# A projection stage with products on zeros before its first chunk, one weight taken in quarters, and the next chunk's transposes one tile later

## The reference

```python
xn = _layernorm(x, axis=-1)                                  # x: (2, 2048, 512), float32
q, k, v = (proj(Wq, bq), proj(Wk, bk), proj(Wv, bv))         # x @ W + bias, 16 heads of 32
scores = jnp.einsum('bhqd,bhkd->bhqk', q, k) / jnp.sqrt(jnp.float32(HD))
scores = jnp.where(causal, scores + bias, jnp.finfo(scores.dtype).min)
ctx = jnp.einsum('bhqk,bhkd->bhqd', softmax(scores), v)
attention = ctx.reshape(b, s, d) @ Wo + bo
logits = (norm_w * (xf * jax.lax.rsqrt(var + EPS))) @ router_w.T      # eight experts, the top two
a = jax.nn.silu(jnp.einsum('td,edf->tef', flat, gate_w)) * jnp.einsum('td,edf->tef', flat, up_w)
y = jnp.einsum('ted,te->td', jnp.einsum('tef,efd->ted', a, down_w), cw) * SCALE
return x + attention + y
```

## Time and profile before

| | |
|---|---|
| median of 3 runs | 1926.42 us (1925.46 to 1926.46) |
| profiled execution | 1924.57 us, of which 1922.8 us are its span from first to last instruction |
| PE busy | 1870.5 us (97%) |
| DVE, ACT, POOL busy | 1506.5 (78%), 1415.9 (74%), 1406.0 us (73%) |
| mean granted PE clock | 0.99 |

### The profile page before, as it was taken

How to read it: one execution, slowest core, us unless ns; L and a number is a source line. 1 busy time by engine, 2 the same in 40 slices (tenths; PEclk the granted TensorE clock), 3 DMA queues, 4 the chain that set the end, 5 groups by cost and what they waited for, 6 DMA issues and landing times. The chain is left out here.

```text
span 1922.8 us, 39426 instructions
## 1 busy us (share of the span) xinstructions
PE 1870.5 (97%) x8656; PEld 1441.3 (75%) x8657; DVE 1506.5 (78%) x3497; ACT 1415.9 (74%) x2790; POOL 1406.0 (73%) x1214
## 2 busy tenths in 40 slices
PE   6999999999999999999999999999998989999997
PEld 5788777777777777777777777777756767888875
DVE  6454466898999989999999998999957956666664
ACT  4333322999999999999999999999972235555554
POOL 5111113899999999999999999999948846666665
PEclk9999999999999999999999999999999999999998
DMA  8577767542423424234242342423217756556553
GB/s 274 199 245 257 270 221 235 143 106 63 107 74 77 106 63 110 71 78 104 63 111 70 79 103 63 119 63 83 77 41 230 251 178 122 103 104 108 104 98 65
DMA packets 119242, 242.14 MB, mean 126 GB/s; under 512 B 17632, under 2 KB 54368, under 8 KB 112896
## 3 DMA queue, kind: packets, MB, share of 16 engines
q1 hardware_dynamic: 101120, 205.84, 36.7%
q0 software_dynamic: 18080, 35.81, 10.2%
HBM read 139.28 MB, written 104.21 MB: 127 GB/s over the span
## 5 line engine op out<-in xcount | busy, mean ns | idle before, releaser
L1175 POOL TENSOR_TENSOR probs_lo<-probs,probs_hi 128x512 fp32r<-128x512 f32 x812 | 1020.2, 1300 | 79.4 <-ACT probs L1210 76.4
L1209 ACT ACTIVATE probs_hi<-s_ps 128x512 fp32r<-128x512 f32 x967 | 680.9, 704 | 26.1 <-DVE s_ps L1282 22.2
L1210 ACT ACTIVATE probs<-s_ps 128x512 f32<-128x512 f32 x933 | 637.5, 702 | 10.2 <-DVE s_ps L1282 6.6
L1261 DVE TENSOR_REDUCE m_part<-m_ps 128x1 f32<-128x512 f32 x744 | 477.8, 682 | 3.0
L1518 PE MATMUL s_ps<-q_st,k_st 100*128 100x512 f32 (+3 forms) x880 | 310.5, 385 | 1.1 <-DMA q_st<-m_rows 0.8
L1502 PE MATMUL m_ps<-k_st,q_st 98*128 98x512 f32 (+2 forms) x840 | 291.1, 382 | 1.3 <-DVE v_raw L776 0.8
L1537 PE MATMUL o_ps<-probs_hi,v_split 128*96 128x512 f32 (+3 forms) x741 | 272.4, 375 | 1.7 <-POOL probs_lo L1175 1.7
L1538 PE MATMUL o_ps<-probs_lo,v_split 128*96 128x512 f32 (+3 forms) x741 | 273.8, 371 | 0.0
L1258 DVE CUSTOM_DVE_ANT_0 m_ps<-m_ps,mask_row 128x128 f32<-128x128 f32 x496 | 244.4, 493 | 16.4 <-PE m_ps L1502 7.8
L1518 PEld LDWEIGHTS s_ps<-q_st,k_st 100*128 100x128 f32 x880 | 162.9, 190 | 61.3 <-ACT probs L1210 22.0
L623 POOL TENSOR_TENSOR v_rows<-v_raw,v_rows 128x512 fp32r<-128x512 f32 x32 | 41.3, 1294 | 228.9 <-ACT v_rows L679 228.9
(11 more groups left out here) (236 smaller groups left out, 3728.3 us busy)
## 6 DMA issues: line engine op xcount, KB each, us to landing
v_d<-v_rows SPq DMA_DIRECT2D x7, 3072.0 KB, 9.4
v_split<-v_d SPq DMA_DIRECT2D x22, 768.0 KB, 8.3
k_st<-k_hi_d SPq DMA_DIRECT2D x44, 256.0 KB
q_st<-q_hi_d SPq DMA_DIRECT2D x44, 256.0 KB
xn_d<-xs SPq DMA_DIRECT2D x8, 1024.0 KB, 11.8
q_hi_d<-qk_hi SPq DMA_DIRECT2D x32, 256.0 KB, 7.7
q_lo_d<-qk_lo SPq DMA_DIRECT2D x32, 256.0 KB, 7.8
k_hi_d<-qk_hi SPq DMA_DIRECT2D x32, 256.0 KB, 3.5
```

The source lines that it names most:

```text
L1175: nc.gpsimd.tensor_tensor(*low_operands(u), ALU.subtract).then_inc(lo_ready_pool, 1)
L1209: nc.scalar.activation(probs_hi[:, P_SLOT[u]], scores, ACT.Exp, scale=SCALE)
L1210: nc.scalar.activation(scores if kind == "Q" else probs[:, P_SLOT[u]], scores, ACT.Exp, scale=SCALE).then_inc(p_ready, 1)
L1261: V.tensor_reduce(top, scores, AX.X, ALU.max).then_inc(m_taken, 1)
```

## The change

Five edits, all in `project`:

1. 30 matmuls of 128x512 on `rw`, which POOL first fills with zeros, stand ahead of everything on PE. They write a `pj` bank that nothing reads before it is overwritten.
2. The identity is loaded ahead of Wq and the other four tables of `consts` behind it.
3. In the first chunk Wq's high and low parts are made in four pieces, ACT's alternating with `x_high`, and the transposes go through x by row blocks, so that a block can start when it is normalised.
4. T0 of each chunk waits for its operands one piece at a time; the two waits at the head of the chunk are gone.
5. In every chunk `transpose_x`, `x_high` and `x_low` of the next chunk stand one tile later: steps 0 to 2 ahead of T5 to T7 and step 3 behind T7.

```diff
+            nc.gpsimd.memset(rw[:, :, :].bitcast(F32), 0.0).then_inc(warm_ready, 1)
             pool.wait_ge(xn_ready, TPC)
-            w_low(0)
+            for k in range(KD):
+                pool.wait_ge(first_hi, k + 1)
+                nc.gpsimd.tensor_tensor(w_lo[:, 0, k], w_raw[:, k], w_hi[0][:, k].bitcast(F32), ALU.subtract).then_inc(first_lo, 1)
+            pool.wait_ge(first_lo, KD)
+            pool.sem_inc(w_split, 1)
             w_low(1)
...
-            w_high(0)
+            act.wait_ge(w_raw_loaded[0], 16)
             for k in range(KD):
+                nc.scalar.activation(w_hi[0][:, k], w_raw[:, k], ACT.Copy).then_inc(first_hi, 1)
                 x_high(0, 0, k, first=True)
...
                 for g in range(2 * G):
-                    if ahead and g >= G:
-                        x_low(c + 1, 1 - par, g - G)
+                    if ahead and g > G:
+                        x_low(c + 1, 1 - par, g - G - 1)
                     beside(g)
                     qk_low(c, g)
...
+                if ahead:
+                    x_low(c + 1, 1 - par, KD - 1)
...
                     for k in range(KD):
+                        if opens and n == 0:
+                            pe.wait_ge(first_hi, k + 1)
+                            pe.wait_ge(xh_ready, KD * c + k + 1)
+                        if opens and n == 1:
+                            pe.wait_ge(xl_ready, 2 + KD * c + k + 1)
+                        if opens and n == 2:
+                            pe.wait_ge(first_lo, k + 1)
...
-            pe.wait_ge(consts_loaded, 16)
-            for k in range(KD):
-                transpose_x(0, 0, k, first=True)
+            pe.wait_ge(warm_ready, 1)
+            for _ in range(WARMING):
+                nc.tensor.matmul(pj[:, BANKS - 1], rw[:, 0], rw[:, :, :].rearrange("p k n -> p (k n)"), start=True, stop=True)
+            pe.wait_ge(ident_loaded, 16)
+            for j in range(TPC):
+                pe.wait_ge(xn_ready, j + 1)
...
             def chunk(c, par, ahead, last=False, first_maxima=((),) * NJ):
-                pe.wait_ge(xl_ready, 2 + KD * (c + 1))
-                pe.wait_ge(w_hi_done, 1)
                 for g in range(2 * G):
-                    if ahead and g >= G:
-                        transpose_x(c + 1, 1 - par, g - G)
+                    if ahead and g > G:
+                        transpose_x(c + 1, 1 - par, g - G - 1)
...
+                if ahead:
+                    transpose_x(c + 1, 1 - par, KD - 1)
                 if not last:
                     router_rows(c, par)
```

More of the change, by code:

```diff
@@ L393, in project @@
     FIRST_BANKS = 3
+    WARMING = 30
     beside = ((0,) * G + (1,) * G + (3,) * TPC, (1, 3, 3, 3, 2, 3, 3, 3, 3, 0, 0, 0))
@@ L457, in project @@
         w_hi_done = sem(ctx, "w_hi_done")
+        warm_ready = sem(ctx, "warm_ready")
+        ident_loaded = sem(ctx, "ident_loaded")
+        first_hi = sem(ctx, "first_hi")
+        first_lo = sem(ctx, "first_lo")
         w_split = sem(ctx, "w_split")
@@ L505, in _ @@
                 sp.dma_start(xs[0][:, j], x[j * P:(j + 1) * P, :]).then_inc(x_first[j], 16)
-            sp.dma_start(consts[:, :, :], t["cst"].rearrange("p (a n) -> p a n", a=5)).then_inc(consts_loaded, 16)
+            cst = t["cst"].rearrange("p (a n) -> p a n", a=5)
+            sp.dma_start(consts[:, 0], cst[:, 0]).then_inc(ident_loaded, 16)
             load_weight(0)
+            sp.dma_start(consts[:, 1:], cst[:, 1:]).then_inc(consts_loaded, 16)
             for dst, src in ((b_col[:, 0], t["bq"]),
@@ L687, in _ @@
             deviation(0)
-            w_high(0)
+            act.wait_ge(w_raw_loaded[0], 16)
             for k in range(KD):
+                nc.scalar.activation(w_hi[0][:, k], w_raw[:, k], ACT.Copy).then_inc(first_hi, 1)
                 x_high(0, 0, k, first=True)
+            act.wait_ge(first_hi, KD)
+            act.sem_inc(w_hi_done, 1)
             w_high(1)
@@ L698, in chunk @@
                 for g in range(2 * G):
-                    if ahead and g >= G:
-                        x_high(c + 1, 1 - par, g - G)
+                    if ahead and g > G:
+                        x_high(c + 1, 1 - par, g - G - 1)
                     qk_high(c, g)
@@ L707, in chunk @@
                         router_root(c + 1)
+                if ahead:
+                    x_high(c + 1, 1 - par, KD - 1)
                 for j in range(TPC):
@@ L915, in maximum_tile, with tile @@
                                  k_st[0][0:ROW_MAX, k0:k0 + w], start=True, stop=True).then_inc(m_scored, 1)
-            def tile(c, g, pairs, maxima=()):
+            def tile(c, g, pairs, maxima=(), opens=False):
                 pe.wait_ge(pj_used, NJ * c + g + 1)
@@ L926, in tile @@
                         maximum_tile(m)
-                    if n == 2 and g == 0:
-                        pe.wait_ge(w_split, 1)
                     for k in range(KD):
+                        if opens and n == 0:
[5 more added lines that the diff above has]
+                            pe.wait_ge(first_lo, k + 1)
                         lhsT, rhs = pairs(k)[n]
@@ L937, in qk_tile @@
                 tile(c, g, lambda k: ((w_hi[w][:, k, cols], x_hi[par][:, k]), (w_hi[w][:, k, cols], x_lo[par][:, k]),
-                                      (w_lo[:, w, k, cols], x_hi[par][:, k])), maxima)
+                                      (w_lo[:, w, k, cols], x_hi[par][:, k])), maxima, opens=g == 0)
             def v_tile(c, par, j, maxima):
@@ L959, in turn_logits @@
                 last.then_inc(r_ready, 1)
-            pe.wait_ge(consts_loaded, 16)
-            for k in range(KD):
-                transpose_x(0, 0, k, first=True)
+            pe.wait_ge(warm_ready, 1)
[4 more added lines that the diff above has]
+                pe.wait_ge(xn_ready, j + 1)
+                for k in range(KD):
+                    last = nc.tensor.transpose(turned_x(k, True)[:, j * P:(j + 1) * P], xs[0][:, j, k * P:(k + 1) * P], ident)
+                    if j == TPC - 1:
+                        last.then_inc(xt_ready, 1)
             def chunk(c, par, ahead, last=False, first_maxima=((),) * NJ):
-                pe.wait_ge(xl_ready, 2 + KD * (c + 1))
-                pe.wait_ge(w_hi_done, 1)
                 for g in range(2 * G):
-                    if ahead and g >= G:
-                        transpose_x(c + 1, 1 - par, g - G)
+                    if ahead and g > G:
+                        transpose_x(c + 1, 1 - par, g - G - 1)
                     if last and g == G:
```

## The result

The changed kernel takes 1941.58 us (median of six runs, 1937.48 to 1943.12), the kernel before on the same chip 1926.53 us. The ratio is 1.0079, with a 95% interval of 1.0067 to 1.0091: slower by 15.05 us, where +8.35 was forecast. The time lies above the upper end of the range, 1938.5. The profiled execution of the changed kernel takes 1943.12 us with a span of 1941.1 us, the slowest of its six.

What follows compares the result with a forecast made beforehand. PE, busy 97% of the span, was taken as the bound. Terms +9.75 (chunks 1 to 5), +0.4 (chunk 6) and -1.8 (chunk 0) sum to +8.35 us: 1934.8 us on the 1926.42 median, range 1930.0 to 1938.5.

Steps and rivals of the forecast that it cites:

- The later transposes: Chunks 1 to 5: new PE waits for x_low behind T7, plus the moved step of transposes, +9.75 us in all.
- keeps its distance from the chunk's start: T5's high part, chunks 1 to 5: it hangs on DMAs issued at the chunk's start, whatever PE does in between.
- Chunk 0, -1.8 us: First chunk: filled stall shortens it, T0's gain lost in a bank wait; -1.8 us, between -3.5 and +2.
- 2.5 us sooner: Chunk 0: T0 ends near 17.7 us instead of 20.19, a gain the prediction said is not kept.
- Step 2's wait: Chunk 0, PE's transposes behind T4: a wait of some 0.5 us for step 0's x_low.
- Chunk 6, +0.4 us: One step of transposes that stood ahead of PE's stall comes behind it, costing +0.4 us.
- keeps its time: Chunk 6: the matmul of the third maximum, at 269.05 us, is not moved, as DVE's slots hold the same passes.
- Nothing in the rest: Behind project: a microsecond gained or lost there goes through to the end, with no term for later stages.
- Ring released sooner: Rival, chunks 1 to 5: stores free the ring earlier, no new wait; about 1925, no change; chance 0.12.
- The clock's falls: Rival: PE's clock falls in the new waits, some 1.7 us each; three falls give 1940; chance 0.08.
- The start loses: Rival, chunk 0: all thirty products cold, T0 ends near 22, chunk at +2 us, 1938.6 in all; chance 0.03.
- Full gain: Rival: T0's and the stall's 2.5 us both kept, no new wait, 1921.4; 0.07 together with much sooner release.

Runs made afterwards that it cites:

- e8: Changed kernel, with SP issuing the load of x behind the stores of tile 3 instead of tile 0: 1927.58 us, ratio 1.0008.
- e3: Changed kernel, with only PE's transposes one tile later; ACT's and DVE's passes back in their old places, DVE's behind the maximum's reduction: 1920.48 us, ratio 0.9972.
- e4: The changed kernel run again without any edit, for a second profiled execution: 1940.18 us, ratio 1.0082.
- e5: Kernel before, with only PE's transposes one tile later and DVE's passes behind the maximum's reduction, without edits 1 to 4: 1917.16 us, ratio 0.9961.
- e2: Changed kernel with edit 5 undone, so edits 1 to 4 alone: 1928.34 us, ratio 1.0013.
- e6: e3 plus two one-column DVE memsets on a spare tile ahead of attend, 988 DVE instructions: 1924.26 us, ratio 0.9999.
- e9: e3 with edit 2 undone, so all tables of consts load ahead of Wq again: 1921.52 us, ratio 0.9966.
- e12: Changed kernel with the load of x behind tile 3's stores and fifteen one-column DVE memsets ahead of attend: 1922.49 us, ratio 0.9981.
- e7: Changed kernel plus fifteen one-column DVE memsets on a spare tile ahead of attend, 1003 DVE instructions: 1936.95 us, ratio 1.0066.

## Why the prediction was wrong in size

The direction was right, and the largest cost stood where it was forecast. The first profiled execution is 15.6 us late near the end of the loop of `attend`, 7.2 more than the forecast of +8.35. Of these 7.2, chunks 1 to 5 are 1.6, chunk 0 is 1.4, chunks 6 and 7 are 1.0, and 3.2 are `attend`, for which there was no term.

**What bounds the kernel.** Right: PE is the bound, and the ring of the q and k stores is tied to PE only through DVE's order. e8 and e3 cut that tie at its two ends, and the wait went each time.

**The later transposes, +9.75 us.** Right in place, sign and growth from chunk to chunk; 10.49 us in e4, 11.32 in the profiled execution of the changed kernel, whose chunk 1 has the clock's fall. The terms for chunks 2 to 5 were each 0.15 to 0.4 us too small. The step behind that is that the ring's release "keeps its distance from the chunk's start". Measured from the router start of the chunk before to T5's high part, that distance is in e4 0.15 us shorter than in the kernel before in chunk 1, and 0.16, 0.18, 0.23 and 0.39 longer in chunks 2 to 5; the terms missed by -0.16, 0.15, 0.17, 0.21 and 0.37. (In the changed kernel's chunk 5, for instance, 243.43 less 204.97 is 38.46, where it was 234.87 less 196.73, or 38.14.) The row at 243.43 names PE and not a store as what ended the wait, but PE had done T5 before 235.8; e4's row at the same place names the store. Why the distance grows isn't shown.

**Chunk 0, -1.8 us.** This step failed. -0.36 in the one execution, -1.37 in the other. The end of the products (10.3), the late T4 and T5 were right within 0.5 us. Three sizes were not.

- "2.5 us sooner" for the end of T0 was 0.89 (0.96 in e4). POOL's quarters end at 17.24 (four passes from 12.26 in 4.98 us), as forecast (17.4). PE is what was late: it got one product per 1.0 us while ACT's passes alternated (12.64 to 15.66), and then the granted clock was at half, 0.66 over 15 to 20 in both executions, a fall that this sum does not have; the four products on `x_lo` take 1.71 us (16.25 to 17.96). In e3 the clock stayed at 1.00 there, and T0 took 5.2 us instead of 6.7. This costs nothing here, since T4 waits for DVE, but it is most of what edits 1 to 4 were to bring.
- "I take 0.5" for the delay of DVE's chain was 0.97 in the first execution (`normalise` at 30.22, 29.25 in the kernel before) and nothing in e4 (29.25). It comes from ACT: its pass over Wk starts at 16.05 instead of 14.57, behind a Wq that landed later and eight alternating passes; in e4, with Wq at 9.77, at 15.31.
- Step 2's wait, "some 0.5 us", was 1.15 (1.11 in e4), since `x_low` of step 0 now stands behind T4's low part and `router_scale`. The first operation of `router_scale` on `newton`, at 37.62, lasts 1.16 us instead of 0.16: it ends at 38.78 and POOL's pass of 37.46 ends at 38.76. So edit 5 put `x_low` behind an operation that POOL holds up.

POOL's pass over Wk does hold `mean_square` as the prediction used it: the DVE operation of 21.06 ends at 22.67, POOL's pass at 22.65, while the median of that operation in the trace is 0.16 us. The Trainium skill (SBUF — State Buffer, Who interferes with whom) has such a pair of engines share a port pair under an exclusive lock; the trace agrees. And e1, with edit 5 alone, gained 1.23 us in chunk 0, e5 2.16: what chunk 0 gained is the filled stall of the earlier trace rows alone. Edits 1 to 4 brought no gain in chunk 0 that an execution shows clearly: 2.30 us later in e2 than before, 0.29 later in e3 than in e5, and the changed kernel 0.87 later and e4 0.14 sooner than e1.

**Chunk 6, +0.4 us.** +1.13 here with 0.28 more in chunk 7; in e4 +2.73, of which 1.4 are the clock's fall behind chunk 5's wait. The step that failed is that the matmul of the third maximum "keeps its time":

```profile
280.78 0.41 PE L933 MATMUL mp<-k_st,q_st 98*128 98x384 f32 x1 [3.46 <-DVE m_part L848]
```

It comes 34.82 us behind chunk 5's router start (245.96), and came 34.05 behind it before (269.05 less 235.00). T4's high part on ACT, which hangs on the same stores, is later by as much (31.21 against 30.43). These 0.77 and the moved step's 0.41 are 1.18, close to the 1.13. The chunk differs by more than that from kernel to kernel, and a fall of the clock inside it goes with the longer ones. Nine executions have one in a window of 5 us between 260 and 285 us (lowest 0.58 to 0.82), the kernel before and the changed one among them; there the chunk takes 42.06 to 44.79 us. In the five without (e2, e5, e6, e9, e12) it takes 40.89 to 41.79.

**Nothing in the rest.** This step failed as well, and it is the largest single miss: the prediction has a microsecond of `project` that "goes through to the end", and no term for anything behind `project`. There the changed kernel loses 3.2 us between 347 and 1412 us, e4 2.8, e1 3.2. e6 and e7 show that it goes with the count of DVE's instructions ahead of the loop, in both directions, whatever these do. Why 988 is worse than 986, 987 and 1003 isn't shown.

**The sum.** Up to the end of the loop: -0.36 + 11.32 + 1.13 + 0.28 + 3.2 = 15.6, all of the measured offset there. Behind it the two executions of the changed kernel stand 18.7 and 13.3 us late at 1897 us, so what the output projection and the experts add or give back there is not told apart from one execution to the next.

**The rivals.** Ring released sooner: it didn't happen by itself, but e8 made it happen, and its forecast of "about 1925, no change" is near e8's 1927.58, which holds the 3 us of `attend` too. (That 1925 has the moved step's 0.4 us in chunk 6 alone; with the 0.41 of each of chunks 1 to 5, which the prediction's own sum has, it would be 1927.) The clock's falls: one behind a new wait in each of the two executions, behind chunk 1's in the first, where the chunk took 0.80 us more, and behind chunk 5's in e4, where the router rows took 1.4 us more; 1.7 was forecast for a fall. By the Trainium skill (TensorE: Matmul & The Clock Gate, Part 1) idle gaps between bursts bring half rate back; behind 1.91 us it did (0.66 in 80 to 85) and behind 2.26 us in e4 (0.72 in 245 to 250), behind 1.52 and 1.00 us in e4's chunk 1 and behind 2.22 us in the first execution's chunk 5 (245.55) it did not, so the gap alone doesn't tell. The start loses: no, the products were not all cold. Full gain: no, since the new waits came.

## What to carry to other kernels

When a step is moved later, move it only on the engine that is the bound; its producers keep their early place, or they get queued behind the very operation that the move was to avoid (e3 and e5 against e1: 20 to 24 us, of which some 3 are the loop of `attend`). Ask of each gap which chain ends last in it: thirty products and quartered passes made T0 end 0.9 us sooner and bought nothing, since T4 waited on a chain that ran past them. Where a difference stands in a stage that wasn't edited, in every turn of a loop alike, try the same kernel with a few idle instructions ahead of it before explaining the difference by the edit.

## What was not expected of the hardware

- A loop whose instructions are unchanged took 103.15 to 103.19 us per turn in the five profiled executions with 988 DVE instructions and 102.84 to 102.92 in the nine with 986, 987 or 1003. One row of waits follows it (11.6 to 12.1 us in 53 to 55 places against 4.8 to 7.0 in 25 to 39).
- The first part of Wq could be worked on at 9.77 to 11.48 us from execution to execution, with either order of loads, a spread of 1.7 us, about what the forecast gave the whole first chunk.
- A DVE operation on 128x4 numbers, 0.16 us elsewhere, lasts until POOL's pass over a weight ends: 1.61 us in the changed kernel and 2.37 before. Another of that size, at 37.62 us, lasts 1.16 us, to the end of a POOL pass on 64x512 numbers.
- In two executions a stall of PE of nearly the same length (2.26 and 2.22 us, at the same place of chunk 5) was followed by half clock in one and by full clock in the other.
